# The x matmuls of a group in one block at count 8, in a graph-sum kernel on one core

## The chip, the core and the metric

The kernel runs on one core of a Trainium2 chip. Its engines run side by side, each with a queue of its own in program order: TensorE (PE, matmuls; PEld is its weight loading), VectorE (DVE), ScalarE (ACT), GpSimd (POOL, here the indirect gathers) and SyncE (SP, plain DMA issues). They wait for one another by semaphores. The metric is the device time of one execution in microseconds (us); the profile is one further execution, taken by the hardware profiler.

## The reference

12500 nodes with 64 features, 400000 edges sorted by their target `dst`. Each edge adds to its target the source's row times one matrix, plus the edge's own 64 attributes times another, both times the edge's weight; the node's own row is added, and each row is normalised.

```python
h = feat_src @ node_w.T
rf = review_feat @ review_w.T
m = (h[src_idx] + rf) * edge_w
out = segment_sum(m, dst_idx, num_segments=N_DST)
x = layernorm(x + out, axis=-1)
```

## The kernel before, in words

The sums are made first and the two matrices are applied once at the end (line 1451). The first edges go by gathering: units of 2048 edges, whose source rows POOL fetches with 16 indirect DMAs each (line 534). The other nodes go by counting: for 128 consecutive edges, a window, DVE makes two one-hot tiles, `hot_key` (line 854, 128x294) and `hot_lo` (line 855, 128x256), in `make_hot`; PE multiplies them into `count_ps` with two matmuls (`count_window`, line 1425), which gives how often (by weight) each source occurs for three target nodes; ACT copies two windows at a time from PSUM into `counts` (`read_counts`, line 1240). For a group of 21 windows PE then multiplies `counts` by the table x in `sum_x`: 98 pieces, two matmul instructions each, 196 in all (line 1438), with outputs in two halves of the array's columns (128x64 tiles). DVE adds the result to `sums` in `add_x` (line 772).

The work is 18 rounds of 6 groups. Every engine runs a hand-written `step_of(at, g)` for each group, as a list of places k. On PE a step makes the 21 counts of the next group, c = g + 1, and between them, at fixed places k: `sum_x` of group g in portions; `sum_g` (64 matmuls in 128x32 tiles, line 1352) and `multiply_g` (line 1381) of a gathered unit in steps 0 to 4; `sum_a` (32 matmuls, line 1352) and `multiply_a` (line 1389) of a unit of edge attributes alone; at place TURN the transposes of the next round's index data (`turn_g`, `turn_a`, `turn_cols`, lines 1319 to 1343) in steps 1, 2 and 4.

The one-hot tiles lie in HOT_BUFS = 6 buffers. DVE's list for a step begins with the place k = 6 and ends with k = 26: it makes windows 6 to 20 of group c and windows 0 to 5 of the group after it, and `make_hot` of window n first waits until window n - 6 is counted:

```python
dve.wait_ge(counted, n - HOT_BUFS + 1)
```

Among the windows DVE has, at k = 9 `make_g_hot`, at 12 `find_rows` (step 0), at 14 `take_src` (step 1), at 15 `add_g` and `make_g_slot_hot`, at 18 `make_a_hot`, at 22 `find_runs` (step 1, line 802 on; it waits for a row that POOL gathers), at 24 `add_a` and `make_a_slot_hot`, at the end `add_x`; at the head of a step `prepare_g` (step 1), `prepare_a` (step 2), `prepare` (step 4, line 816 on). `count_ps` has two buffers of two windows, so PE waits for ACT before a third pair. PE's `sum_x` of group g waits until group g's counts are all copied and until `add_x` of group g - 1 is done. `each_round` is a loop of 8 passes of two rounds, and two rounds written out.

Of the kernel before, what the change touches and what calls it, by code (L numbers as in the profile page):

```python
# [37 lines left out]
GATHERED = 5  # L38
# [3 lines left out]
ATTR_BUFS = 2  # L42
NOWHERE = 1000.0

PIECES_FROM, PIECES_UNTIL = 3, 19
SUM_G, MULTIPLY_G, SUM_A, MULTIPLY_A, TURN = 1, 8, 10, 17, 6

def build(nc, x, src, dst, attr, weight, node_w, review_w, out):
    NODES, F = x.shape
# [45 lines left out]
    with ExitStack() as ctx:  # L95
# [264 lines left out]
        def is_narrow(eng):  # L360

            return eng.value_load(flag_tab[0:1, 0:1], min_val=0, max_val=1)
# [21 lines left out]
        def windows_of(at, g):  # L384

            return SPILLS if isinstance(at.r, int) and at.r == ROUNDS - 1 and g == RG else GW

        def a_units(at):

            return LAST_A if isinstance(at.r, int) and at.r == ROUNDS - 1 else SUMMED  # L390
# [9 lines left out]
        def is_last(at):  # L400

            return isinstance(at.r, int) and at.r == ROUNDS - 1
# [788 lines left out]
        def _(act):  # L1191
# [13 lines left out]
            def read_cols(q, p, n=RW):  # L1205

                act.wait_ge(turned, q + 1)
                act.activation(cols[p][:, :, 0:n], turn_ps[:, 0:CELLS * n].rearrange("p (q t) -> p q t", q=CELLS), ACT.Copy
                               ).then_inc(cols_ready, 1)

            def compare(q):

                if not isinstance(q, int) or q >= 1:
                    act.wait_ge(row_ready, q)
                act.activation(compared[:, :], sample_tab[0:RW, :], ACT.Sign, bias=bias_all[:, bass.ds(q, 1)],
                               accum_out=less[:, 0:1]).then_inc(compared_all, 1)

            def copy_g(at, i):

                u = at.r * GATHERED + i  # L1220
                act.wait_ge(g_summed, u + 1 + GATHERED)
                act.wait_ge(g_multiplied, u + 1)
                act.activation(g_slots[:, :], g_slots_ps, ACT.Copy).then_inc(g_copied, 1)
# [8 lines left out]
            def read_counts(at, g, e):  # L1232

                n = min(2, windows_of(at, g) - 2 * e)
                act.wait_ge(counted, first(at, g) + (2 * e + n))
                no = group_no(at, g)
                if e == 0 and (not isinstance(no, int) or no >= 1):
                    act.wait_ge(x_summed, no)
                to = counts[:, g % 2, :, 2 * e * D:(2 * e + n) * D].rearrange("p h (a d) -> p a h d", d=D)
                act.activation(to, count_ps[(g + e) % 2][:, 0:n, 0:KEYS].rearrange("p a (h d) -> p a h d", d=D), ACT.Copy  # L1240
                               ).then_inc(counts_read, 1)
# [18 lines left out]
            with act.If(is_narrow(act) == 1):  # L1260
                read_cols(0, 0)
                for e in range(EVACS):
                    read_counts(Round(0, 0), 0, e)

                def step_of(at, g):

                    last = is_last(at)
                    c = g + 1
                    evacs = (windows_of(at, c) + 1) // 2
                    for e in range(EVACS):  # L1270
                        if e < evacs:
                            read_counts(at, c, e)
                        if e == 0 and g < GATHERED:
                            copy_g(at, g)
                        if e == 2 and g == 0 and not last:
                            compare(at.r + 1)
                        if e == 3:
                            if g == 1 and not last:
                                read_g(at.r + 1, 1 - at.p)
                            if g == 2 and not last:  # L1280
                                read_a(at.r + 1, 1 - at.p)
                            if g == 4 and not last:
                                read_cols(at.r + 1, 1 - at.p)
                            if g == 3 and last:
                                read_cols(at.r + 1, 1 - at.p, SPILLS)
                        if e == 5 and g < a_units(at):
                            copy_a(at, g)

                def round_of(at):

                    for g in range(RG):
                        step_of(at, g)

                each_round(act, round_of)
# [17 lines left out]
        def _(pe):  # L1312
# [171 lines left out]
            with pe.If(is_narrow(pe) == 1):  # L1484
                for k in range(GW):
                    count_window(Round(0, 0), 0, k)
                pe.wait_ge(x_tab_loaded, 32 if NODES % P else 16)

                def step_of(at, g):

                    last = is_last(at)
                    c = g + 1
                    windows = windows_of(at, c)
                    spots = PIECES_UNTIL - PIECES_FROM
                    for k in range(GW):
                        if k == SUM_G and g < GATHERED:
                            sum_g(at, g)
                        if k == TURN:
                            if g == 1 and not last:
                                turn_g(at.r + 1)  # L1500
                            if g == 2 and not last:
                                turn_a(at.r + 1)
                            if g == 4 and not last:
                                turn_cols(at.r + 1)
                            if last and g == 0:
                                pe.wait_ge(spill_totals, 1)
                                pe.wait_ge(cols_ready, ROUNDS)
                                pe.matmul(turn_ps[0:RW, 0:1], tri[:, :], rank[:, 0, ROUNDS - 1:ROUNDS],
                                          start=True, stop=True)
                                pe.matmul(turn_ps[0:1, 1:2], rank[:, 0, ROUNDS - 1:ROUNDS], all_ones[0:RW, 0:1],  # L1510
                                          start=True, stop=True).then_inc(spill_ranked, 1)
                            if last and g == 1:
                                pe.wait_ge(spill_chosen, 1)
                                for a in range(2):
                                    pe.matmul(turn_ps[0:SPILLS, a:a + 1], spill_of[:, a, :], all_ones[0:RW, 0:1],
                                              start=True, stop=True)
                                pe.matmul(turn_ps[0:1, 2:2 + SPILLS], all_ones[0:RW, 0:1], spill_of[:, 1, :],
                                          start=True, stop=True)
                                pe.matmul(turn_ps[0:1, 2 + SPILLS:3 + SPILLS], all_ones[0:RW, 0:1], lane_bad[:, :],
                                          start=True, stop=True).then_inc(spill_found, 1)  # L1520
                            if last and g == 3:
                                turn_cols(ROUNDS, SPILLS)
                            if last and g == 4:
                                pe.wait_ge(spill_checked, 1)
                                pe.wait_ge(cols_ready, ROUNDS + 1)
                                pe.matmul(turn_ps[0:1, 0:1], spill_b[:, 1:2], all_ones[0:SPILLS, 0:1],
                                          start=True, stop=True).then_inc(spill_bad, 1)
                        if k == MULTIPLY_G and g < GATHERED:
                            multiply_g(at, g)
                        if k == SUM_A and g < a_units(at):  # L1530
                            sum_a(at, g)
                        if k == MULTIPLY_A and g < a_units(at):
                            multiply_a(at, g)
                        if PIECES_FROM <= k < PIECES_UNTIL:
                            n = k - PIECES_FROM
                            sum_x(at, g, range(n * HI // spots, (n + 1) * HI // spots))
                        if k < windows:
                            count_window(at, c, k)

                def round_of(at):  # L1540

                    for g in range(RG):
                        step_of(at, g)

                each_round(pe, round_of)
                sum_x(Round(ROUNDS - 1, 1), RG, range(HI), SPILL_NS)
# [31 lines left out]
```

## Time and profile before

| | |
|---|---|
| median of three runs (range) | 2459.62 us (2455.4 to 2465.33) |
| the profiled execution | 2467.1 us, span 2465.4 us |
| PE busy | 2227.3 us, 90% |
| PEld busy | 1743.4 us, 71% |
| DVE busy | 2039.8 us, 83% |
| ACT busy | 977.7 us, 40% |
| POOL busy | 1591.8 us, 65% |
| mean granted clock of TensorE | 0.942 of full speed |

Busy time is the time in which an engine has any instruction in flight. On PE it holds the fill and drain of the array, so 90% is not 90% of what the array could do. The granted clock is 1.00 at 2.4 GHz and 0.50 at 1.2 GHz.

### The profile page before, as it was taken

Reading aid. Unit: us, or ns where it says so; the run is one execution under the profiler, and the core shown is the slowest. Engines: PE = TensorE matmul, PEld = TensorE weight load, DVE = VectorE, ACT = ScalarE, POOL = GpSimd, SP = SyncE. Lnnn points to the kernel's source line nnn. Section 1 sums busy time; section 2 is a strip of 40 time slices with the busy share of each in tenths; the row PEclk is TensorE's granted clock in tenths of the full one; section 3 lists DMA queues with packets and bytes.
Section 4 is the critical chain, followed back from the end, with each engine's and each line's share of the span. In section 5 each row is a group of like instructions: output and inputs, shape, how many; then the busy total and the mean of one; then the engine's idle time right before and its main releaser. Section 6 shows DMA issues by size and latency. Waiting matters only on the chain.

```text
span 2465.4 us, 93210 instructions
## 1 busy us (share of the span) xinstructions
PE 2227.3 (90%) x35999; PEld 1743.4 (71%) x36000; DVE 2039.8 (83%) x6206; ACT 977.7 (40%) x1602; POOL 1591.8 (65%) x1539
## 2 busy tenths in 40 slices
PE   1779989999899989998999899989998999999983
PEld 1557767777677767776777677767776777777773
DVE  3958977888798978887888788978888888898974
ACT  0324433344344434443444344434443344444434
POOL 4777674757575757676676757674767576767400
PEclk7779988999999989998999999989999899999996
DMA  6223333333333323332333333333333333333202
GB/s 131 55 63 74 75 65 67 63 76 71 74 74 68 79 59 79 70 79 62 75 73 77 74 73 73 77 66 68 75 77 66 71 74 76 73 77 68 56 3 53
DMA packets 480104, 173.08 MB, mean 70 GB/s; under 512 B 443549, under 2 KB 455397, under 8 KB 479445
## 3 DMA queue, kind: packets, MB, share of 16 engines
q1 hardware_dynamic: 426791, 111.57, 21.0%
q0 software_dynamic: 49632, 51.95, 10.7%
q8 instruction: 314, 5.14, 0.9%
q10 hardware_dynamic: 3218, 3.20, 0.7%
q14 instruction: 149, 1.22, 0.2%
HBM read 163.39 MB, written 3.20 MB: 68 GB/s over the span
## 4 chain that ended last, share of the span: by engine, by line
PE 82%; DVE 5%; issue 4%; POOL 3%; ACT 3%; DMA 1%; DVEq 1%; ACTq 0%; SPq 0%; POOLq 0%
PE count_ps L1425 37%; PE x_ps L1438 35%; PE unit_ps L1352 6%; POOL rows L534 3%; ACT counts L1240 2%; DVE hot_lo L855 2%; DVE hot_key L854 1%; PE window_bank L1389 1%; DMA counts<-dst 1%; PE window_bank L1381 1%; DVE sums L772 1%; ACT x_tab L1308 1%; DMA dst_row<-dst,row_i 0%; DVEq L759 0%; PE turn_ps L1343 0%
## 5 line engine op out<-in xcount | busy, mean ns | idle before, releaser
L534 POOL DMA_INDIRECT rows<-x,g_src_cols x1440 | 1506.5, 1046 | 676.1 <-issue 431.1
L1240 ACT ACTIVATE counts<-count_ps 128x588 f32<-128x588 f32 (+1 forms) x1192 | 879.4, 749 | 1371.4 <-PE count_ps L1425 1371.4
L1425 PE MATMUL count_ps<-hot_key,hot_lo 128*128 128x294 f32 x4552 | 1165.6, 351 | 113.7 <-ACT counts L1240 57.3
L855 DVE SCALAR_TENSOR_TENSOR hot_lo<-count,cols 128x256 fp32r<-128x256 f16 x2276 | 1083.8, 476 | 0.0
L1438 PE MATMUL x_ps<-counts,x_tab 128*64 128x63 f32 x21364 | 1055.0, 233 | 21.1 <-DVE sums L772 20.6
L854 DVE TENSOR_SCALAR hot_key<-count,cols 128x294 fp32r<-128x294 f16 x2276 | 867.8, 381 | 241.4 <-PE count_ps L1425 215.5
L1438 PEld LDWEIGHTS x_ps<-counts,x_tab 128*64 128x64 f32 x21364 | 815.6, 140 | 289.8 <-issue 235.7
L1425 PEld LDWEIGHTS count_ps<-hot_key,hot_lo 128*128 128x128 f32 x4552 | 692.5, 194 | 270.7 <-ACT counts L1240 73.0
L1352 PE MATMUL unit_ps<-rows,g_hot 128*32 128x64 f32 x5760 | 106.8, 229 | 15.6 <-issue 15.6
L1352 PEld LDWEIGHTS unit_ps<-rows,g_hot 128*32 128x32 f32 x5760 | 91.6, 115 | 32.2 <-issue 32.2
L662 POOL TENSOR_TENSOR x_tab<-x_tab,counts 128x512 f32<-128x512 f32 (+1 forms) x6 | 5.5, 936 | 123.8 <-DVE counts L1021 123.8
L1352 PE MATMUL unit_ps<-rows,a_hot 128*32 128x64 f32 x3392 | 72.9, 229 | 0.0
L1352 PEld LDWEIGHTS unit_ps<-rows,a_hot 128*32 128x32 f32 x3392 | 55.1, 114 | 19.0 <-issue 19.0
L772 DVE TENSOR_TENSOR sums<-sums,x_ps 64x63 f32 (+1 forms) x216 | 47.0, 218 | 14.9 <-PE x_ps L1438 7.8
L762 DVE TENSOR_TENSOR sums<-sums,window_bank 64x128 f32 x106 | 31.0, 292 | 20.9 <-issue 19.4
L1389 PE MATMUL window_bank<-a_slot_hot,a_slots 128*64 128x128 f32 x212 | 45.9, 298 | 0.0
L753 DVE TENSOR_TENSOR sums<-sums,window_bank 128x128 f32 x90 | 26.0, 289 | 13.3 <-issue 12.2
L552 POOL DMA_INDIRECT dst_row<-dst,row_i x18 | 19.1, 1061 | 27.6 <-DVE row_i L796 23.0
L1381 PE MATMUL window_bank<-g_slot_hot,g_slots 128*128 128x128 f32 x180 | 36.0, 282 | 0.0
L1451 PE MATMUL count_ps<-w_t,sums 128*128 128x128 f32 x196 | 24.1, 289 | 12.7 <-DVEq L1187 12.7
L744 DVE TENSOR_SCALAR a_slot_hot<-column,a_slot_dst 128x128 f32<-128x128 f32 x106 | 32.3, 305 | 3.5
L1389 PEld LDWEIGHTS window_bank<-a_slot_hot,a_slots 128*64 128x64 f32 x212 | 20.4, 135 | 18.0 <-issue 18.0
(196 smaller groups left out, 697.3 us busy)
## 6 DMA issues: line engine op xcount, KB each, us to landing
rows<-edge_attr SPq DMA_DIRECT2D x196, 512.0 KB
rows<-x,g_src_cols POOLq DMA_INDIRECT x1440
out<-x_tab SPq DMA_DIRECT2D x12, 256.0 KB
counts<-dst SPq DMA_DIRECT2D x1, 848.0 KB
a_stage<-dst SPq DMA_DIRECT2D x17, 48.0 KB
a_stage_w<-edge_weight SPq DMA_DIRECT2D x17, 48.0 KB
g_stage<-src SPq DMA_DIRECT2D x18, 40.0 KB
g_stage<-dst SPq DMA_DIRECT2D x18, 40.0 KB
```

The source lines that it names most:

```text
L534: pool.indirect_dma_start(out=g_x[:, i, t, :], out_offset=None, in_=x, in_offset=bass.IndirectOffsetOnAxis(ap=g_src_cols[at.p][:, k:k + 1] ...
L744: dve.tensor_scalar(a_slot_hot[:, :], column[:, :], a_slot_dst[at.p][:, i:i + 1], None, ALU.is_equal).then_inc(a_slot_hot_made, 1)
L762: dve.tensor_tensor(sums[F:2 * F, bass.ds(base, WIN)], sums[F:2 * F, bass.ds(base, WIN)], a_window_ps, ALU.add).then_inc(added, 1)
L772: made = dve.tensor_tensor(to, to, x_ps[half * F:(half + 1) * F, 0:NS], ALU.add)
L854: dve.tensor_scalar(hot_key[h][:, :], count16[:, :], cols_[:, KEY, j:j + 1], None, ALU.is_equal)
L855: dve.scalar_tensor_tensor(hot_lo[h][:, :, :], count16[:, 0:P].unsqueeze(1).to_broadcast([P, 2, P]), cols_[:, LO, j:j + 1], cols_[:, W_LOW ...
L1240: act.activation(to, count_ps[(g + e) % 2][:, 0:n, 0:KEYS].rearrange("p a (h d) -> p a h d", d=D), ACT.Copy).then_inc(counts_read, 1)
L1352: done = pe.matmul(to[j * PAD:(j + 1) * PAD, :], hot[:, at:at + PAD], tiles[:, q * QUADS + j, :], start=(q == 0), stop=(q == STACK - 1))
L1381: pe.matmul(g_window_ps, g_slots[:, :], g_slot_hot[:, :], start=True, stop=True).then_inc(g_multiplied, 1)
L1389: pe.matmul(a_window_ps, a_slots[:, :], a_slot_hot[:, :], start=True, stop=True).then_inc(a_multiplied, 1)
L1425: done = pe.matmul(count_ps[(g + e) % 2][:, k % 2, 0:KEYS], hot_lo[h][:, i, :], hot_key[h][:, :], start=(i == 0), stop=(i == 1))
L1438: done = pe.matmul(x_ps[half * F:(half + 1) * F, 0:n], x_tab[:, hi, :], counts[:, g % 2, hi, 0:n], start=(hi < 2), stop=(hi >= HI - 2))
```

## The change

On PE the 196 x matmuls of a group no longer stand in 16 portions at places 3 to 18 but all together at place 8, ahead of count 8. `sum_g` goes from place 1 to 4 and `sum_a` from 10 to 12, `multiply_a` from 17 to 16, and the transposes from 6 to 8; `multiply_g` stays at 8. On ACT `copy_g` goes behind the second copy of counts instead of the first. DVE's, POOL's and SP's lists stay as they are.

```diff
-PIECES_FROM, PIECES_UNTIL = 3, 19
-SUM_G, MULTIPLY_G, SUM_A, MULTIPLY_A, TURN = 1, 8, 10, 17, 6
+PORTIONS_AT = (8,)
+SUM_G, MULTIPLY_G, SUM_A, MULTIPLY_A, TURN = 4, 8, 12, 16, 8
...
-                        if e == 0 and g < GATHERED:
+                        if e == 1 and g < GATHERED:
                             copy_g(at, g)
...
-                    spots = PIECES_UNTIL - PIECES_FROM
+                    spots = len(PORTIONS_AT)
...
-                        if PIECES_FROM <= k < PIECES_UNTIL:
-                            n = k - PIECES_FROM
+                        if k in PORTIONS_AT:
+                            n = PORTIONS_AT.index(k)
                             sum_x(at, g, range(n * HI // spots, (n + 1) * HI // spots))
```

## Rows read from the trace of the kernel before

**Rows 1.** Part 4 of the page: engines' shares of the chain that ended last.

```profile
PE 82%; DVE 5%; issue 4%; POOL 3%; ACT 3%; DMA 1%; DVEq 1%; ACTq 0%; SPq 0%; POOLq 0%
```

**Rows 2.** Busy time by stretch, two rounds: us, PE PEld DVE ACT POOL, clock, DMA, GB/s.

```profile
916.30:1038.50 122.20, 117.62 (x1984) 91.83 (x1980) 108.97 (x335) 52.54 (x84) 87.83 (x84) 1.00 0.36 75
1038.50:1172.40 133.90, 124.74 (x1982) 97.45 (x1981) 109.49 (x336) 52.63 (x84) 88.65 (x84) 0.92 0.33 70
```

**Rows 3.** Timeline of PE at full clock: start us, us, engine, line, operation, [idle before].

```profile
1037.41 1.10 PE L1352 MATMUL unit_ps<-rows,g_hot 128*32 128x64 f32 x64
1038.44 0.81 PE L1425 MATMUL count_ps<-hot_key,hot_lo 128*128 128x294 f32 x4
1039.18 0.57 PE L1438 MATMUL x_ps<-counts,x_tab 128*64 128x63 f32 x12
1039.67 0.54 PE L1425 MATMUL count_ps<-hot_key,hot_lo 128*128 128x294 f32 x2
1040.14 0.57 PE L1438 MATMUL x_ps<-counts,x_tab 128*64 128x63 f32 x12
```

**Rows 4.** The same timeline in the last step, which has only eight counts.

```profile
2389.36 4.05 PEld L1438 LDWEIGHTS x_ps<-counts,x_tab 128*64 128x64 f32 x136 [0.17 <-issue]
```

**Rows 5.** Timeline of PE where the transposes stand between a count and a portion.

```profile
116.82 0.54 PE L1425 MATMUL count_ps<-hot_key,hot_lo 128*128 128x294 f32 x2
...
117.89 0.57 PE L1438 MATMUL x_ps<-counts,x_tab 128*64 128x63 f32 x12
```

**Rows 6.** Timeline of all engines: a count and the window of DVE that waits for it.

```profile
1005.43 0.53 PE L1425 MATMUL count_ps<-hot_key,hot_lo 128*128 128x294 f32 x2
...
1006.00 0.37 DVE L854 TENSOR_SCALAR hot_key<-count,cols 128x294 fp32r<-128x294 f16 x1 [0.19 <-PE count_ps L1425]
```

**Rows 7.** Timeline of DVE in a stretch of 19 windows that waits for nothing.

```profile
1097.84 0.40 DVE L854 TENSOR_SCALAR hot_key<-count,cols 128x294 fp32r<-128x294 f16 x1
...
1100.07 0.47 DVE L772 TENSOR_TENSOR sums<-sums,x_ps 64x63 f32 x2
1100.46 0.29 DVE L816 TENSOR_SCALAR off<-run_dst,b_all 126x128 f32<-126x128 int32 x1
...
1102.73 0.37 DVE L854 TENSOR_SCALAR hot_key<-count,cols 128x294 fp32r<-128x294 f16 x1
...
1114.76 0.36 DVE L854 TENSOR_SCALAR hot_key<-count,cols 128x294 fp32r<-128x294 f16 x1
```

**Rows 8.** Timeline of DVE: from the first instruction of `find_runs` to the next window.

```profile
1054.04 0.28 DVE L802 TENSOR_SCALAR off<-dst_row,b_all 126x128 f32<-126x128 int32 x1
...
1055.12 0.37 DVE L854 TENSOR_SCALAR hot_key<-count,cols 128x294 fp32r<-128x294 f16 x1
```

**Rows 9.** Groups of POOL from 100 to 2394 us: busy us, mean ns | idle before.

```profile
L534 POOL DMA_INDIRECT rows<-x,g_src_cols x1391 | 1457.8, 1048 | 656.5 <-issue 416.5 <-DVE g_src_cols L706 237.3 <-DVE row_i L796 2.7
```

**Rows 10.** Timeline of PE: counts in succession, ahead of a lower clock.

```profile
339.17 1.09 PE L1425 MATMUL count_ps<-hot_key,hot_lo 128*128 128x294 f32 x6 [0.59 <-ACT counts L1240]
341.26 0.71 PE L1438 MATMUL x_ps<-counts,x_tab 128*64 128x63 f32 x12 [1.00 <-DVE sums L772]
```

**Rows 11.** Busy time of PE by stretch: us, PE busy (x), clock, DMA, GB/s.

```profile
341.00:342.00 1.00, 0.74 (x13) 0.77 0.14 33
...
2412.00:2416.00 4.00, 3.23 (x15) 0.50 0.02 6
2416.00:2417.00 1.00, 1.00 (x7) 0.58 0.00 0
```

**Rows 12.** The same for all engines (order as in rows 2), counting alone.

```profile
80.00:85.00 5.00, 5.00 (x17) 3.63 (x15) 5.00 (x16) 2.92 (x4) 3.78 (x5) 0.50 0.12 21
```

**Rows 13.** Timeline of PE at half clock.

```profile
90.10 1.93 PE L1352 MATMUL unit_ps<-rows,g_hot 128*32 128x64 f32 x64
91.96 1.35 PE L1425 MATMUL count_ps<-hot_key,hot_lo 128*128 128x294 f32 x4
93.24 0.91 PE L1438 MATMUL x_ps<-counts,x_tab 128*64 128x63 f32 x12
```

## The prediction, made before the changed kernel ran

> **What bounds the kernel now.** I read first the page's chain of work that ended last: PE holds 82% of it, DVE 5% [rows 1]. So PE sets the pace, and the question is whether it works or fills and drains. Second, two stretches of one round each, from `add_x` to `add_x`: 122.2 us at full clock, 133.9 us for one with the end of a loop pass in it, where the clock is 0.92 [rows 2]. A step is thus 122.2 / 6 = 20.4 us. DVE is busy in 109 of the 122.2 us: it is close behind PE, and that decides this case. Third, PE's timeline at full clock [rows 3]. From a portion to the next portion 0.96 us pass: 0.49 from x to the count, 0.47 from the count to x. Two counts in succession and the way to x take 0.74 us, so a count that follows a count costs 0.27. Fourth, a long row of x matmuls in the last step: 136 weight loads in 4.05 us [rows 4], 0.0298 us each. Twelve of them should take 0.36 us and a count 0.27, 0.63 together; they take 0.96. Each portion pays 0.33 us for going over from one shape of tile to the other and back.
>
> **What the change takes from PE.** One block costs 196 x 0.0298 = 5.84 us, sixteen portions at 0.49 cost 7.84, and 15 counts fall from 0.47 to 0.27: 15 x 0.33 = 5 us less per step on PE. If PE alone were late, a step would go to some 15.4 us. It isn't alone.
>
> **What takes PE's place.** While the block runs PE counts nothing, and DVE can only fill the six one-hot buffers: windows 8 to 13. Window 14 waits until count 8 is done, and count 8 stands behind the block. Behind that waiting instruction lie all of DVE's other work and every later window. Now PE's block needs window 7 of the next group counted, and DVE makes that one 15 windows after it was released. So there is a closed ring for each step, and I add it up:
> - count 8 starts, window 14 starts 0.57 us later [rows 6];
> - DVE makes windows 14 to 20, 0 to 5 and 6, 7. In a stretch that waits for nothing, 18 window periods take 16.92 us in all [rows 7]. `prepare` is 2.27 of it (1100.46 to 1102.73) and `add_x` some 0.5 (0.39 between the rows, plus the end of the window ahead of it). `make_g_hot`, `add_g` with its one-hot and `make_a_hot`, two instructions each as `add_x` has, I put at 0.5 each. That leaves 12.65 / 18 = 0.70 us per window. Fourteen periods and the last window's whole length, 0.76, are 10.56 us;
> - between them stand `add_g` 0.5, `make_a_hot` 0.5, `add_a` with its one-hot 0.65 (an estimate: as `add_x`, plus reading its address), `add_x` 0.5: 2.15 us. `make_g_hot`, `find_rows` and `take_src` fall into the time of the block and cost nothing as long as the block is longer than DVE's 6 x 0.70 + 0.5 = 4.7 us, which it is;
> - from count 7 to x 0.47, with `multiply_g` between them some 0.69. The trace has transposes in that place: 1.07 us [rows 5], that is 0.60 more than nothing. `multiply_g` has two instructions against their seven, so it lies between 0 and 0.60; I take 0.22;
> - the block with the way to count 8: 5.84.
>
> The sum is 0.57 + 10.56 + 2.15 + 0.69 + 5.84 = 19.8 us. Over a round, step by step: 6 x 19.8 = 118.8; plus `find_runs` 1.08 [rows 8], `prepare` 2.27, `prepare_g` and `prepare_a` some 0.65 each (an estimate from `prepare`'s twelve instructions, they have four and three), and three sets of transposes that now stand between count 7 and the block, 3 x 0.60 = 1.8; less `add_g` and `multiply_g`, which step 5 has not, 0.7. That is **124.6 us, against 122.2 now**. The 5 us that PE is spared are paid out as DVE standing still in the block (5.84 + 0.69 + 0.57 less 4.7, about 2.4 us) and as PE standing idle between DVE's windows. Over 17.75 rounds (the last step has only 8 counts): +2.4 x 17.75 = +43 us.
>
> What else moves: `sum_g` at place 4 and `sum_a` at 12 stand between counts that wait for DVE anyway; at full clock they fit there, since `sum_g` is 1.03 us [rows 3] and windows 4 to 7 follow only 0.7 us apart, with `add_x` among them. `copy_g` behind the second copy is needed only at place 8. The transposes' inputs come from the step's head, long before. POOL's gathers and SP's loads follow `sum_g` and `sum_a`, two or three windows later than before. POOL needs 80 gathers of 1.05 + 0.30 us a round, 108 us, with four more for rows and runs 113 [rows 9]; a round of 124 us leaves it 11. So these edits I cost at nothing; if that cover failed, POOL's 113 us would be the floor, not an addition.
>
> The ends of loop passes, 8 of them, cost 11.7 us each now (133.9 less 122.2), part of it the stop, part the interleaved work that follows at half clock. A dense block gets the clock back sooner; I keep 6 us and book 8 x 5.7 = -46 us. Bounds: 0 and -94.
>
> **The clock.** In the new step the stretch from count 16 to `sum_g` is PE at DVE's pace: a count of 0.27 us every 0.70, for some 6 us, four or five counts in any 3 us. The trace shows what such thin work does. At 337.5 to 341.3 us PE made six counts, waited 0.59, made six more and waited 1.00 [rows 10]; the clock fell to 0.50 just then (0.77 in that microsecond) [rows 11], though no gap was above 1.0 us. And at the start, where PE counts at DVE's pace with nothing between, it stays at 0.50 throughout [rows 12]. So I expect it to fall in most steps and to return only in the block or in `sum_g`: when the last matmuls began at 2412.77 it was back after about 4 us of dense work [rows 11]. What this costs, from rows at half clock [rows 13]: `sum_g` to count 1.86 us against 1.03, two counts to x 1.28 against 0.74, `multiply_g` and the way to x some 0.5 more; less about 0.5 that PE had to spare. That is 1.4 us in steps with `sum_g` (0 and 3), some 1.0 in steps 1 and 2, where DVE's `prepare_g` and `prepare_a` hide a part. In steps 4 and 5 a thin stretch (2.27 us of `prepare`, or no `sum_g`) comes right ahead of the block, and the block begins at half clock: 4 us at half speed lose 2 us, 2.2 with the way there. A round: 2.8 + 2.0 + 4.4 = 9.2, say 10 us with a block that begins slow now and then. The thin stretch is only about as thin as the row that fell, so I count six tenths: 6 x 17.75 = **+110 us**; bounds 0 and 14 x 17.75 = 250.
>
> The Trainium skill, page "TensorE: Matmul & The Clock Gate", section "Why this matters for your kernels", says that drops in the middle of a kernel come from idle gaps of PE between bursts of matmuls, longer than any that the new step has. By that rule the clock would stay at full, which is rival B below. The fall at 341 us, after gaps of 0.59 and 1.00 us, speaks against it.
>
> **The sum.** Profiled execution 2467.1 + 43 - 46 + 110 = 2574 us. The profiled execution stands 7.5 us above the median of the runs, so 2566; I predict 2565.
>
> **The rivals.**
> - A, the forecast: the ring of DVE and block, with a clock that falls in most steps: 2500 to 2680, 2565. Chance 0.66.
> - B, the clock stays: 2467 + 43 - 46, less 7 = 2457; with the loop ends wholly won back 2410, with 0.68 us a window (42 us less) some 2415. No change, or a little faster. It decides if thin counting doesn't count as idle. For it: between 74 and 95 us the array was at half clock already, which shows no fall. Against it: rows 10 and 11. Chance 0.22.
> - C, not slower by far: DVE isn't held in the block, because windows are built ahead elsewhere. Then PE's 5 us come through, until POOL's 113 us a round is the floor: (122.2 - 113) x 17.75 = 163 us, with the loop ends 94: about 2205. It needs DVE to be more than six windows ahead, which `make_hot`'s wait forbids. Chance 0.08, for what I may have read wrongly of that wait.
> - D, the clock falls and doesn't return within the block: 5.84 us become some 10 in every step, 4 x 107 = 430 on top: 3000. Dense work brought it back within 4 us elsewhere. Chance 0.04.
>
> That the change doesn't do what it says would mean that the block is broken up by a wait; its first matmul needs `add_x` of the group before, which DVE does two windows ahead of window 7, so I see none.
>
> **How the numbers follow.** The likeliest is A. The range takes B's upper half and A: 2420 to 2680; C, D and the low end of B are left out, about 0.18. About 0.5% is what a measurement of this kernel can tell from no change (2447 to 2472). Slower: A 0.66 and D 0.04, 0.70. B divides into 0.12 no change and 0.10 faster; with C faster is 0.18.
>
> **What would show it.** Right: in the profile after, x stands as 196 matmuls in 5.8 us or a little more; DVE waits before window 14 in every step, 2 to 3 us, for count 8; PE's share of the chain falls and DVE's rises far above 5%; the granted clock falls from 0.94 to some 0.8, and the timeline of a single step has PE at 0.50 between counts 20 and 4. The rounds are 125 us where the clock holds, 130 or more where it falls. Wrong: steps below 19 us (C); mean clock at 0.94 or above (B); a block of 10 us (D); DVE without waits at window 14, which would overthrow the ring itself.

## The result, and the profile after

The changed kernel takes 2555.9 us (median of 4 runs, 2553.8 to 2564.8), the kernel before, run beside it, 2460.2 us: a ratio of 1.040, 95% interval 1.037 to 1.042. It is slower by 96 us; 2565 was predicted. The profiled execution's span is 2552.8 us, its mean granted clock 0.82 (before 2465.4 us and 0.942).

The chain of work that ended last answers to [rows 1]:

```profile
PE 48%; DVE 32%; issue 10%; DVEq 4%; POOL 3%; DMA 1%; ACT 1%; ACTq 0%; SPq 0%; POOLq 0%
```

PE has gone from 82% to 48%, DVE from 5% to 32%. The path now passes to and fro between the two. The waits of the changed kernel say where (engine, line <- what was waited for: us in total, times, longest):

```profile
DVE hot_key L854 <- PE count_ps L1425: 406.6, 111, 6.3
POOL rows L534 <- DVE g_src_cols L706: 299.2, 17, 21.8
...
PE count_ps L1425 <- DVE hot_lo L855: 215.8, 344, 16.6
```

The same three waits of the kernel before:

```profile
DVE hot_key L854 <- PE count_ps L1425: 215.5, 594, 3.3
POOL rows L534 <- DVE g_src_cols L706: 242.2, 17, 23.6
PE count_ps L1425 <- DVE hot_lo L855: 36.1, 8, 16.6
```

DVE now waits once in each step, 406.6 / 111 = 3.7 us, instead of often and briefly, and PE waits for DVE's windows 344 times instead of 8. The next two views show one such pair. PE's timeline of a step (start us, us, engine, line, operation [idle before]), which answers to [rows 3] and [rows 13]:

```profile
1305.17 0.38 PE L1381 MATMUL window_bank<-g_slot_hot,g_slots 128*128 128x128 f32 x2
1305.48 5.93 PE L1438 MATMUL x_ps<-counts,x_tab 128*64 128x63 f32 x196
1311.34 1.35 PE L1425 MATMUL count_ps<-hot_key,hot_lo 128*128 128x294 f32 x8
...
1316.73 1.14 PE L1425 MATMUL count_ps<-hot_key,hot_lo 128*128 128x294 f32 x4 [0.72 <-DVE hot_lo L855]
1318.09 2.89 PE L1425 MATMUL count_ps<-hot_key,hot_lo 128*128 128x294 f32 x8 [0.22 <-DVE hot_lo L855]
1321.37 0.86 PE L1425 MATMUL count_ps<-hot_key,hot_lo 128*128 128x294 f32 x2 [0.39 <-DVE hot_lo L855]
1322.16 1.94 PE L1352 MATMUL unit_ps<-rows,g_hot 128*32 128x64 f32 x64
...
1327.25 5.93 PE L1438 MATMUL x_ps<-counts,x_tab 128*64 128x63 f32 x196
```

And DVE's timeline beside the block, same columns; the third row is window 13, the last that the six buffers hold, the fourth window 14:

```profile
1302.86 0.47 DVE L772 TENSOR_TENSOR sums<-sums,x_ps 64x63 f32 x2
...
1305.34 0.26 DVE L715 TENSOR_TENSOR g_hot<-column,g_cols 128x112 f32<-128x112 f32 x1
...
1308.91 0.37 DVE L854 TENSOR_SCALAR hot_key<-count,cols 128x294 fp32r<-128x294 f16 x1
...
1311.93 0.37 DVE L854 TENSOR_SCALAR hot_key<-count,cols 128x294 fp32r<-128x294 f16 x1 [2.25 <-PE count_ps L1425]
```

The block stands in one piece: 5.86 us from its first matmul to count 8 (1305.48 to 1311.34). DVE is through with window 13 at 1309.7, waits 2.25 us, and begins window 14 0.59 us after count 8 began (0.57 in [rows 6]). Then PE's counts follow DVE, up to the next block at 1327.25.

PE's granted clock over that step (stretch, us, PE busy, clock, DMA share, GB/s; compare [rows 11]):

```profile
1314.90:1318.00 3.10, 2.18 (x10) 1.00 0.86 183
1318.00:1319.00 1.00, 0.76 (x3) 1.00 0.01 2
1319.00:1320.00 1.00, 0.93 (x4) 0.80 0.00 0
1320.00:1321.00 1.00, 0.91 (x3) 0.50 0.00 0
...
1324.00:1325.00 1.00, 1.00 (x8) 0.50 0.00 0
1325.00:1326.00 1.00, 1.00 (x6) 0.50 0.43 100
1326.00:1327.00 1.00, 1.00 (x10) 0.79 1.25 284
```

While PE counts at DVE's pace its clock drops from 2.4 to 1.2 GHz (at 1319.6), and it is back at 1326.4, after `sum_g` and four counts in succession. In that stretch `sum_g` takes 1.94 us, not the 1.10 of [rows 3]. The clock record of this trace has 107 stretches at half clock after the first 80 us, 860 us together, and every step, from one block to the next, has some time at half clock; before, there were 13 stretches, 228 us together.

Two rounds (stretch, us, busy PE PEld DVE ACT POOL, clock, DMA share, GB/s), which answer to [rows 2]:

```profile
1455.60:1584.90 129.30, 115.94 (x1980) 95.69 (x1979) 107.00 (x337) 52.13 (x85) 86.90 (x84) 0.85 0.34 71
1584.90:1722.30 137.40, 119.26 (x1981) 98.16 (x1979) 106.58 (x336) 52.79 (x85) 88.29 (x84) 0.82 0.33 67
```

The second holds the end of a loop pass. Over ten rounds in succession from the middle of each span, five with a loop end and five without: without, 122.2 us before and 129.3 to 132.3 after, mean 131.4; with one, mean 133.2 before and 134.8 after. What a round loses in its steps is partly won back at the loop ends.

### The profile page after: what moved, and what is told of

Its sections match the earlier page's. It is cut to its first block, busy times and chain, and to the rows that moved or that the text cites. A ratio compares the mean times of both kernels' runs of the same rounds, so it can differ in the third digit from the quotient of the medians.

```text
span 2552.8 us, 93210 instructions
## 1 busy us (share of the span) xinstructions
PE 2167.8 (85%) x35999; PEld 1790.6 (70%) x36000; DVE 1984.4 (78%) x6206; ACT 973.7 (38%) x1602; POOL 1610.2 (63%) x1539
## 4 chain that ended last, share of the span: by engine, by line
PE 48%; DVE 32%; issue 10%; DVEq 4%; POOL 3%; DMA 1%; ACT 1%; ACTq 0%; SPq 0%; POOLq 0%
PE x_ps L1438 26%; DVE hot_lo L855 16%; PE count_ps L1425 14%; DVE hot_key L854 10%; PE unit_ps L1352 5%; POOL rows L534 3%; DVE sums L762 1%; DVEq L759 1%; PE window_bank L1381 1%; DMA counts<-dst 1%; DVEq L750 1%; DVE a_hot L715 1%; DVEq L853 1%; ACT x_tab L1308 1%; DMA dst_row<-dst,row_i 0%
## 5 line engine op out<-in xcount | busy, mean ns | idle before, releaser
L534 POOL DMA_INDIRECT rows<-x,g_src_cols x1440 | 1523.7, 1058 | 732.9 <-issue 427.9
L1425 PE MATMUL count_ps<-hot_key,hot_lo 128*128 128x294 f32 x4552 | 1149.6, 380 | 294.5 <-DVE hot_lo L855 215.8
L1240 ACT ACTIVATE counts<-count_ps 128x588 f32<-128x588 f32 (+1 forms) x1192 | 860.2, 748 | 1351.1 <-PE count_ps L1425 1348.9
L1425 PEld LDWEIGHTS count_ps<-hot_key,hot_lo 128*128 128x128 f32 x4552 | 794.7, 226 | 587.9 <-DVE hot_lo L855 248.4
L854 DVE TENSOR_SCALAR hot_key<-count,cols 128x294 fp32r<-128x294 f16 x2276 | 858.5, 377 | 415.8 <-PE count_ps L1425 406.6
L1438 PE MATMUL x_ps<-counts,x_tab 128*64 128x63 f32 x21364 | 693.2, 230 | 0.8 <-DVE sums L772 0.7
L1438 PEld LDWEIGHTS x_ps<-counts,x_tab 128*64 128x64 f32 x21364 | 678.0, 146 | 18.7 <-issue 9.3
L1352 PE MATMUL unit_ps<-rows,g_hot 128*32 128x64 f32 x5760 | 171.7, 310 | 0.0
L1352 PEld LDWEIGHTS unit_ps<-rows,g_hot 128*32 128x32 f32 x5760 | 150.4, 169 | 24.8 <-issue 24.8
L1223 ACT ACTIVATE g_slots<-unit_ps 128x128 f32<-128x128 f32 x90 | 24.9, 277 | 104.2 <-PE unit_ps L1352 104.2
```

What stands on the lines that cost most here:

```text
L534: pool.indirect_dma_start(out=g_x[:, i, t, :], out_offset=None, in_=x, in_offset=bass.IndirectOffsetOnAxis(ap=g_src_cols[at.p][:, k:k + 1] ...
L854: dve.tensor_scalar(hot_key[h][:, :], count16[:, :], cols_[:, KEY, j:j + 1], None, ALU.is_equal)
L1352: done = pe.matmul(to[j * PAD:(j + 1) * PAD, :], hot[:, at:at + PAD], tiles[:, q * QUADS + j, :], start=(q == 0), stop=(q == STACK - 1))
L1425: done = pe.matmul(count_ps[(g + e) % 2][:, k % 2, 0:KEYS], hot_lo[h][:, i, :], hot_key[h][:, :], start=(i == 0), stop=(i == 1))
L1438: done = pe.matmul(x_ps[half * F:(half + 1) * F, 0:n], x_tab[:, hi, :], counts[:, g % 2, hi, 0:n], start=(hi < 2), stop=(hi >= HI - 2))
```

## The experiments

Four theories had to be told apart: that the new order closes a ring between DVE's six buffers and the block; that the clock's falls come on top; that PE's own matmuls or the moved sums cost something by themselves; that DVE as a whole, or POOL, is the bound. All times are medians; behind them stands the ratio to the kernel before, run beside each, with its 95% interval.

### The clock: keep PE dense between the counts

One more matmul ahead of each count in the stretch in which PE goes at DVE's pace, into columns of PSUM that nobody reads:

```diff
+filler_ps = unit_ps[:, 3 * F:3 * F + 256]
...
+if k > MULTIPLY_A or k < (SUM_G if g <= GATHERED else 8):
+    pe.matmul(filler_ps, hot_lo[h][:, 0, :], hot_key[h][:, 0:256], start=True, stop=True)
 for i in range(2):
     done = pe.matmul(count_ps[...][:, k % 2, 0:KEYS], hot_lo[h][:, i, :], hot_key[h][:, :], ...)
```

> The changed kernel with one more matmul of 256 columns (on the window's own one-hot tiles, into unused columns of the unit_ps bank, read by nobody) ahead of the two of each count from place 17 to place 3 (to 7 ahead of a step 5), where PE waits for DVE. Work is added, none taken. Theory A (the thin counting lets TensorE's clock fall, and that costs some 110 us on top of the ring of block and one-hot windows): the granted clock returns from 0.82 to 0.93 or above and the time falls by 80 to 130 us, to 2425 to 2475. Rival B (only the ring of DVE and block sets the time; the lower clock falls into time that PE has to spare): the clock may return but the time stays at 2556 within 15 us. Rival E (PE is late in the thin stretch): slower, above 2570.

Measured: 2468.1 us (2462.3 to 2481.3), 1.005 (1.003 to 1.008), mean clock 0.956. PE got 940 more matmuls and the kernel became 88 us faster. A round (columns as above), a block on PE's timeline, and DVE's wait in the same step:

```profile
1406.90:1533.50 126.60, 111.54 (x2034) 91.88 (x2032) 106.65 (x336) 52.45 (x85) 88.03 (x84) 0.97 0.35 73
```

```profile
1283.18 0.43 PE L1382 MATMUL window_bank<-g_slot_hot,g_slots 128*128 128x128 f32 x2
1283.54 5.93 PE L1441 MATMUL x_ps<-counts,x_tab 128*64 128x63 f32 x196
1289.41 1.35 PE L1428 MATMUL count_ps<-hot_key,hot_lo 128*128 128x294 f32 x8
```

```profile
1289.98 0.37 DVE L855 TENSOR_SCALAR hot_key<-count,cols 128x294 fp32r<-128x294 f16 x1 [2.99 <-PE count_ps L1428]
```

So the falls cost at least 88 us. The rounds without a loop end are 126.2 to 126.6 us: this is the ring at (nearly) full clock, against 122.2 before. The block is the same 5.9 us and DVE still waits, 2.99 us in this step and 326.0 / 113 = 2.9 us in the mean: what stays is the ring, and with it alone the change brings nothing.

### The ring: one more buffer, with the slow clock and without

Seven buffers for the one-hot tiles (some small tables share memory with another tile to make room), in the changed kernel, in the one with the extra matmuls, and in the kernel before:

```diff
-HOT_BUFS = 6
+HOT_BUFS = 7
...
```

> The changed kernel with seven one-hot buffers instead of six (three small tiles of the last round share the room of another to make place); the same instructions. Theory A: DVE gets one more window done during the block, so the ring from count 8 to the next block is one window shorter: 0.70 us a step, 107 steps, 75 us: 2480 (2465 to 2500). DVE's wait ahead of the window after the block falls from 3.7 to 3.0 us a step. Rival (the block and the half clock on PE set the time, DVE only follows): 2556 within 15 us, and DVE's wait stays.

> The changed kernel with both seven one-hot buffers and the extra matmuls that keep PE dense. The extra matmuls are work that the reference doesn't need. Theory A: the two prices are separate, the clock's is already off in the run with the extra matmuls (2468), and one more window of 0.70 us per step comes off the ring: 6 x 0.70 x 17.75 = 75 us, so 2393, range 2370 to 2420, clock at 0.95. Rival (the seventh buffer's gain of 102 us came mostly by the clock, which rose from 0.82 to 0.87 with it): 2440 to 2470.

> The kernel before with seven one-hot buffers instead of six. Theory A (the ring of DVE and block): a seventh buffer pays only where PE stops counting for long; in the interleaved kernel DVE's waits for a buffer are off the path, so the time stays: 2460 us, 2445 to 2475. Rival (a buffer is worth some 100 us in any order, so the gain of the seventh in the changed kernel says nothing of the block): 2355 to 2400.

Measured: 2453.8 us (1.000, 0.998 to 1.003) in the changed kernel, 102 us less, where 75 were expected; 2377.9 us (0.969, 0.966 to 0.972) with the extra matmuls, 90 us less than without the seventh buffer; 2425.3 us (0.987, 0.985 to 0.990) in the kernel before, where nothing was expected: 31 us less, so that this expectation was wrong. A buffer is thus worth 31 us in the interleaved order too, and 60 to 70 us more where there is a block; one window's 0.70 us x 6 x 17.75 = 75 is the right size for the latter. The two prices add up nearly: 102 us for the buffer alone and 88 for the clock alone make 190, both together bring 178; the missing part may be clock, since with the seventh buffer alone the mean clock rose to 0.867; no run shows this by itself. DVE's wait in the changed kernel with seven buffers:

```profile
DVE hot_key L854 <- PE count_ps L1425: 322.5, 114, 4.7
```

It is 406.6 - 322.5 = 84 us less. In the kernel before, the rounds without a loop end take 121.4 us with the seventh buffer, not 122.2, which is 14 of the 31 us; the rest lies in the rounds with a loop end (130.3 in the mean of the same five, not 133.2).

### The ring: the same work of DVE at two places

Two instructions more on DVE in each step, behind the block (ahead of window 20, shown here) or beside it (the same with 10 in place of 20):

```diff
...
+if k == 20:
+    dve.tensor_scalar(spare_key[:, :], count16[:, 0:224], cols_[:, KEY, j:j + 1], None, ALU.is_equal)
+    dve.scalar_tensor_tensor(spare_lo[:, :, :], count16[:, 0:P]..., cols_[:, LO, j:j + 1], ...)
 dve.tensor_scalar(hot_key[h][:, :], count16[:, :], cols_[:, KEY, j:j + 1], None, ALU.is_equal)
```

> The changed kernel with two more instructions on DVE in each step, shaped like those of a window (224 and 256 columns, into spare tiles that nobody reads), ahead of window 20, that is behind count 8 and ahead of the block. Theory A (closed ring of DVE and block): all of it lies in the ring: 6 x 0.70 x 17.75 = 75 us, 2631, range 2605 to 2670. Rival (DVE isn't what paces the step, the slow clock alone does): 2545 to 2575.

> The same two instructions ahead of window 10, which DVE makes while the block runs and before it stops to wait for count 8. Theory A: they come out of DVE's wait (3.7 us a step by its mean) and cost nothing: 2556, range 2545 to 2575. Rival (DVE's work as a whole is the bound): as ahead of window 20, some 2630.

Measured: 2638.2 us (1.074, 1.068 to 1.079) ahead of window 20, 82 us more than the changed kernel, at nearly the same mean clock (0.815); 2550.5 us (1.039, 1.033 to 1.046) ahead of window 10, no change. DVE's waits, first of the kernel with the work at 20, then of the one with it at 10:

```profile
DVE hot_key L861 <- PE count_ps L1432: 433.3, 112, 7.4
```

```profile
DVE hot_key L861 <- PE count_ps L1432: 344.9, 114, 5.7
```

The two instructions take 0.27 and 0.47 us, 108 times: some 80 us of DVE's time, or 75 if the pair takes a window's 0.70 us. At window 10 they come out of the wait (62 us less than 406.6), at window 20 they go into the end. This shows the ring most directly, and it shows that DVE's sum of work isn't the bound.

### The moved sums: block and places, each alone

The block with the old places of `sum_g`, `sum_a`, `multiply_a`, the transposes and `copy_g`; the block with `sum_g` alone back at place 1 (`SUM_G = 1`, all else as in the changed kernel); the 16 portions with the new places. The edits of the first and of the last:

```diff
 PORTIONS_AT = (8,)
-SUM_G, MULTIPLY_G, SUM_A, MULTIPLY_A, TURN = 4, 8, 12, 16, 8
+SUM_G, MULTIPLY_G, SUM_A, MULTIPLY_A, TURN = 1, 8, 10, 17, 6
...
-                        if e == 1 and g < GATHERED:
+                        if e == 0 and g < GATHERED:
```

```diff
-PORTIONS_AT = (8,)
+PORTIONS_AT = tuple(range(3, 19))
```

> Only the first part of the change: the block at place 8, but the units' sums, the transposes and ACT's copy at their places of before (1, 10, 17, 6, first copy). Theory A: the slowdown is the block's. The transposes at place 6 stand outside the ring: 1.8 us a round less, -32 us. But sum_g at place 1 leaves windows 2 to 7 as a thin stretch right ahead of the block, which then begins at half clock in all steps and not only in two: some 1 us in four steps of six, +60 us. Together 2560 to 2610. Rival (the moved units' sums cause the slowdown, the block alone is harmless or a gain): 2460 or below.

> The changed kernel with sum_g alone back at count 1. Theory A (sum_g's 64 matmuls at count 4 are dense work right ahead of the block and keep its clock up; ahead of count 4 they leave a thin stretch of six counts before it): a block of 196 takes longer in the mean, above 6.6 us instead of 6.2, and the kernel 20 to 50 us more, 2575 to 2610. Rival (what made the old places slower was sum_a at count 10 or the transposes at count 6): 2556, block 6.2 us.

> The changed kernel with the x matmuls back in 16 portions at counts 3 to 18, the sums at their new places 4 and 12. Theory A (the block is what costs): 2460 us, 2440 to 2485, clock 0.94, DVE's wait for count_ps back at some 200 us. Rival (the later sums, by POOL's later gathers, cost something of their own): above 2500, with POOL's wait for g_src_cols above 300 us.

| us (medians) | sums at old places | sums at new places |
|---|---|---|
| 16 portions | 2460 (before) | 2550.5 (sixteen) |
| one block | 2593.6 (oldplaces) | 2555.9 (after) |

With intervals: oldplaces 1.058 (1.052 to 1.064), sixteen 1.042 (1.037 to 1.047); `sum_g` alone at place 1 (sumg1) 2634.6, 1.072 (1.069 to 1.076). The two parts don't add: the new places cost 90 us with portions and bring 38 us with the block. Oldplaces came out as expected. Sixteen (2440 to 2485 expected) and sumg1 (2575 to 2610) did not: sixteen took the time that its rival gave, and `sum_g` alone cost 79 us where 20 to 50 were expected, although the block grew as forecast.

With the block: what `sum_g` at 4 brings is the clock of the block. The weight loads of x in all blocks (busy us, mean ns), in the changed kernel, in oldplaces and in sumg1:

```profile
L1438 PEld LDWEIGHTS x_ps<-counts,x_tab 128*64 128x64 f32 x21364 | 678.0, 146 | 18.7 <-issue 9.3
```

```profile
L1438 PEld LDWEIGHTS x_ps<-counts,x_tab 128*64 128x64 f32 x21364 | 745.5, 158 | 23.6 <-issue 20.7
```

```profile
L1438 PEld LDWEIGHTS x_ps<-counts,x_tab 128*64 128x64 f32 x21364 | 742.6, 157 | 23.2 <-issue 19.4 <-ACT counts L1240 0.5
```

Over 108 blocks that is 6.3 us a block after, 6.9 in the other two. In oldplaces one that begins at half clock looks so:

```profile
1319.85 1.14 PE L1425 MATMUL count_ps<-hot_key,hot_lo 128*128 128x294 f32 x4 [0.89 <-ACT counts L1240]
1320.83 0.38 PE L1381 MATMUL window_bank<-g_slot_hot,g_slots 128*128 128x128 f32 x2
1321.14 7.48 PE L1438 MATMUL x_ps<-counts,x_tab 128*64 128x63 f32 x196
```

Its mean clock is higher than that of the changed kernel (0.862 against 0.82) and it is slower all the same: here the half clock lies in the blocks (250 us of it, against 99 in the changed kernel), and these are on the path. Of sumg1's 79 us, 65 are in the block; the rest isn't divided further.

With the portions: PE's waits of sixteen, and one of them on its timeline:

```profile
PE x_ps L1438 <- DVE sums L772: 101.4, 100, 2.3
PE count_ps L1425 <- ACT counts L1240: 56.3, 95, 0.7
```

```profile
1728.68 1.08 PE L1425 MATMUL count_ps<-hot_key,hot_lo 128*128 128x294 f32 x6 [0.59 <-ACT counts L1240]
1730.75 0.57 PE L1438 MATMUL x_ps<-counts,x_tab 128*64 128x63 f32 x12 [0.98 <-DVE sums L772]
```

The first portion, at place 3, waits 1 us for `add_x` of the group before. In the kernel before this wait is there only 21 times (20.6 us), one of them in [rows 10]. The same portions two places later:

```diff
-PORTIONS_AT = tuple(range(3, 19))
+PORTIONS_AT = tuple(range(5, 21))
```

> The x matmuls in 16 portions, but at counts 5 to 20 instead of 3 to 18, the sums at their new places. Theory A (with sum_g at place 4 make_g_hot holds DVE, add_x comes later, and the first portion at place 3 waits for it: 101 us of PE's waits in the run with 16 portions at 3 to 18): two places later the first portion no longer waits: 2450 to 2490. Rival (it is POOL's later gathers, or the sums' places as such): 2535 to 2555.

Measured: 2357.7 us, 0.960 (0.956 to 0.965), clock 0.974: 193 us less than sixteen and 4% faster than the kernel before, more than was expected. The largest of PE's waits in this kernel are

```profile
PE count_ps L1425 <- issue: 35.0, 14, 3.3
PE count_ps L1425 <- DVE hot_lo L855: 33.4, 4, 16.6
```

Both waits are gone, the 101 us for `add_x` and the 56 for ACT (which the kernel before has too, 57): the last portions at places 19 and 20 stand where PE waited for ACT's copies of the last counts. A round is 118.0 us here. That run's rival, POOL's gathers or the places as such, is out. Why the wait for `add_x` grew in sixteen, the traces tell by the steps in which it stands. In the kernel before it stands in all 18 steps 5, which have no `sum_g`, and only 3 times elsewhere; in sixteen, where no step has `sum_g` ahead of the first portion, in 89 of the 90 steps 1 to 5 and in 11 of the 18 steps 0. So with `sum_g` at place 1 its 1.03 us lie ahead of the portion and cover the wait. What the expectation names instead, `make_g_hot` held by the later `sum_g`, is in sixteen's trace too (35 us, 40 times), but less often than the wait (100 times). No run moved `sum_g` alone among the portions.

### Two blocks of half the size

```diff
-PORTIONS_AT = (8,)
+PORTIONS_AT = (6, 14)
```

> The changed kernel with the x matmuls in two portions of 98 instructions, at places 6 and 14, instead of one of 196 at place 8. Theory A: a portion of 2.9 us, with 1.0 us for the way there and back, is no longer than the 4.2 us in which DVE fills six buffers; DVE is then held nowhere and PE keeps 14/15 of what it was spared. The time is that of DVE's own work, some 110 to 114 us a round, or POOL's 113: 2467 - 9 x 17.75 - 40 = 2270, up to 2350 where the clock still falls. Rival (what made the change slow is the coming together of x as such, or the places of the units' sums): 2460 or above. Rival C of the prediction (PE's switching was not worth 0.33 us a portion): about 2460.

> Two portions at counts 6 and 14 and seven one-hot buffers. Theory A (POOL is already the bound of the run with two portions: 67% of its chain, no wait for g_src_cols left, rounds of 111 us): the buffer brings little, 2265, range 2245 to 2282. Rival (DVE's ring still paces it): 75 us less, 2200.

Measured: 2277.2 us, 0.928 (0.925 to 0.930), clock 0.913; with seven buffers 2262.2 us, 0.921 (0.916 to 0.925), 15 us less. A half block, two of DVE's waits and the chain of the kernel with two portions and six buffers:

```profile
1398.93 3.13 PE L1438 MATMUL x_ps<-counts,x_tab 128*64 128x63 f32 x98
```

```profile
DVE hot_key L854 <- PE count_ps L1425: 51.6, 72, 3.4
DVE off L802 <- DMA dst_row<-dst,row_i: 91.7, 15, 21.2
```

```profile
POOL 67%; issue 20%; DVE 6%; PE 4%; DMA 2%; ACT 1%; DVEq 0%; POOLq 0%; ACTq 0%; SPq 0%
```

A block of 3.1 us is shorter than the six windows, 4.2 us, that DVE can make beside it. DVE's wait for counts falls from 406.6 to 51.6 us, and now POOL's gathers are the chain: POOL's wait for DVE's `g_src_cols` falls from 299.2 to 4.6 us, and DVE waits for a row that POOL gathers instead (`off`). Rounds without a loop end take 109 to 111 us, those with one 121 to 127; over two rounds, 234.5 us, POOL makes 170 gathers, one every 1.38 us. That the seventh buffer, worth 102 us in the changed kernel, brings 15 here speaks for POOL as the bound too. How much of the gain over one block comes from the shorter hold and how much from the two new places, no run divides.

## Why the prediction was right, and where its steps were not

**The ring** is right in its mechanism: closed by DVE's wait for count 8, it takes up work behind count 8 at full price and work beside the block for nothing. Its size was too small. Booked were 124.6 us a round, +43 us; with the extra matmuls the rounds are 126.4, 4.2 x 17.75 = +75 us (the extra matmuls' own time is in it). DVE's wait, put at 2 to 3 us, is 2.25 where the sum had 2.4 and 2.99 in a step with transposes, as 0.6 more for these gives; its mean is 2.9 with the extra matmuls and 3.7 without them, so the rest of it goes with the half clock, which the estimate of the wait left out. The 1.8 us a round by which the sum is short lie in two of its terms. Over the five rounds without a loop end, in the kernel with the extra matmuls, DVE needs 81.4 us a round from the start of window 14 to the end of window 7 (booked 80.4), and from there to the block's first matmul 6.4 us pass (booked 5.7); the blocks, 35.2, and the ways from count 8 to window 14, 3.5, are within 0.2 us of the sum.

**The clock** falls, and for the reason that rows 10 and 11 gave: counting at DVE's pace, with gaps of 0.72, 0.22 and 0.39 us in the step shown, takes it to 1.2 GHz in each step. (Rows 10 were misread: `x6` are six matmuls, that is three counts, and not six, on either side of the gap.) Rival B, no fall, is out; its time of 2457 is near what the kernel takes when the clock is kept (2468), with the first two of the errors named below in it. (Its variant with 0.68 us a window books 42 us; with the ring's 14 periods a step it is 30.) The term was +110, the runs give 88: 131.4 - 126.4 = 5.0 us a round, not six tenths of 10 but five. The size came out near, but its parts did not. Booked, ahead of the six tenths, were 4.0 us for two blocks that begin at half clock, those of steps 4 and 5, and 5.2 for slow sums, counts and ways to the block. In the five rounds the blocks cost 2.9 us more than with the extra matmuls (38.16 against 35.23): step 5's began at half clock each time (7.7 us each), step 4's in only two of five. The way from window 7 to the block costs 2.3 us more (8.7 against 6.4), and from window 14 to window 7 nothing is lost (81.3 against 81.4): a slow count there seems to fit into the time that DVE needs for a window (0.58 us each behind `sum_g` in the step shown, a window 0.70). The Trainium skill's page "TensorE: Matmul & The Clock Gate", section "Why this matters for your kernels", lets drops come from idle gaps between bursts, longer than any in the step shown. There the clock fell with no gap above 0.72 us, and with PE busy for 0.76 and 0.93 of the microseconds around the fall, so here the measurement decides against that rule as the only cause.

**The loop ends** were booked at -46; the rounds give (133.2 - 122.2) - (134.8 - 131.4) = 7.6 us less per loop end, 8 x 7.6 = -61. In the kernel with the extra matmuls a loop end costs much the same, 129.5 - 126.4 = 3.1 us. No run tested this term by itself.

The three measured terms make 75 - 61 + 88 = +102 us, against 96 found. That the forecast of +107 came so near is luck: errors of 32, 15 and 22 us offset each other.

**What was costed at nothing** is the step that failed. `sum_g` at place 4 with the rest isn't free: together they save 38 us with the block, as dense work ahead of it, and cost 90 with portions, where `sum_g` no longer lies ahead of the first one. Rows 10 showed that wait of 1.00 us; the prediction read it only for the clock. POOL's gathers did wait longer for DVE (299 us in the whole span, against 242 before), but POOL's share of the chain is 3% as in [rows 1]: there nothing was lost.

**Rival C** needed DVE not to be held by the block. It was held here; with two half blocks it isn't, and the price given for that case, 2205 with POOL's 113 us a round as the floor, compares with 2262 to 2277. POOL's price per gather was right (1.05 + 0.30 booked, 1.38 found), but POOL gathers across the loop ends too, so that no 94 us were left to win there. **D** is out: a block is 6.3 us in the mean, 7.7 in step 5, and 6.9 in the mean of the two kernels where the clock hits it most.

**What would show it**: 196 matmuls in 5.9 us, DVE's wait before window 14 in every step, PE's share of the chain down and DVE's up, clock 0.82, rounds of 129 and more: as said. Rounds of 125 where the clock holds were to be seen in no stretch of the changed kernel; it fell in every step.

## What to carry to other kernels

Gathering one engine's work into a block spares it the changes of shape, but holds up the engine whose buffers it stops emptying: compare the block's length with what the buffers let the other engine make meanwhile (here 5.9 us against 6 x 0.70), and keep the block shorter than that; two half blocks took 2277 us where one took 2556 and sixteen portions 2460, or 2358 at better places. A place in a hand-written order was not free here: ask for each moved piece which wait it covered where it stood, and which one it covers where it goes. A stretch in which PE follows another engine cost twice here, by its waits and by the clock of the block behind it; dense work between the two took off a part of the second (99 us of half clock in the blocks instead of 250).

## What the hardware showed that was not expected

More matmuls made the kernel faster: 940 of them took 88 us away. A mean clock tells little by itself: 0.862 went with 2593.6 us and 0.82 with 2555.9; in the one 250 of its 716 us at half clock lay inside the blocks, in the other 99 of 921. And the kernel before, with PE at 82% of its chain, had room left: with the portions two places later (and the sums at their new places) it takes 4% less.
